# Causal mask in the last attention: two mask products on TensorE, or an addition on VectorE inside the row maximum

## The reference

```python
h = _rms(x, ln_w)
q = (h @ wq).reshape(B, S, NHEADS, HEAD_DIM); k = (h @ wk)...; v = (h @ wv)...
q, k = _rope(q, k)
scores = jnp.einsum('bqhd,bkhd->bhqk', q, k) / np.float32(np.sqrt(HEAD_DIM))
causal = jnp.tril(jnp.ones((S, S), bool))
scores = jnp.where(causal[None, None], scores, jnp.float32(-1e+30))
attn = jax.nn.softmax(scores, -1)
o = jnp.einsum('bhqk,bkhd->bqhd', attn, v).reshape(B, S, NHEADS * HEAD_DIM)
x = x + o @ wo
```

## Time and profile before

| | us |
|---|---|
| median of 3 runs | 4997.76 |
| lowest, highest | 4989.64, 5001.94 |
| span of the profiled execution | 4945.7 |
| what lies around the span (median less span) | 52.1 |
| PE, DVE, ACT, POOL busy in the span | 4241.6, 3176.8, 1929.8, 1642.4 |

### The profile page before, as it was taken

One profiled execution on the slowest core, in us unless ns is written; L12 is line 12 of the kernel. 1 busy time (PEld: TensorE's weight loads), 2 busy tenths in 40 slices (PEclk: granted clock), 3 DMA queues, 4 the chain that ended last, 5 costly groups with the idle time before them and its releaser, 6 DMA issues.

```text
span 4945.7 us, 68678 instructions
## 1 busy us (share of the span) xinstructions
PE 4241.6 (86%) x23426; PEld 2553.3 (52%) x23426; DVE 3176.8 (64%) x7341; ACT 1929.8 (39%) x4485; POOL 1642.4 (33%) x1384
## 2 busy tenths in 40 slices
PE   3698988888888895998858999999999999949985
PEld 1444544444454443775534555555555555547774
DVE  6788788878778775557635576666757666522223
ACT  0244435344443552322214455545555555511111
POOL 1000000000000002435004464546556554648885
PEclk6799999899999997999989999999999999979998
DMA  3211221211122106773041111111111111058888
GB/s 101 25 31 30 32 44 18 40 31 31 31 32 40 18 9 179 202 186 92 15 161 39 42 44 38 43 47 35 42 39 44 38 47 39 19 153 205 209 205 225
DMA packets 332115, 358.51 MB, mean 72 GB/s; under 512 B 177326, under 2 KB 257862, under 8 KB 330902
## 3 DMA queue, kind: packets, MB, share of 16 engines
q1 hardware_dynamic: 280888, 276.81, 21.6%
q0 software_dynamic: 47984, 76.34, 7.7%
q10 hardware_dynamic: 2898, 0.98, 0.1%
HBM read 212.35 MB, written 81.89 MB: 59 GB/s over the span
## 4 chain that ended last, share of the span: by engine, by line
PE 60%; DVE 22%; DMA 7%; ACT 4%; issue 3%; POOL 2%; SPq 1%; ACTq 0%; DVEq 0%; POOLq 0%
PE PS L2119 7%; DVE a_mm L1265 6%; PE PS L2104 6%; PE PS L2151 6%; PE PS L2134 5%; DMA e_xg<-hrow,e_mt 5%; PE PS L2161 4%; PE PS L914 3%; PE PS L854 2%; PE PS L1611 2%; PE PS L2122 2%; PE PS L881 2%; PE PS L719 2%; PE PS L2578 2%; PE PS L892 1%
## 5 line engine op out<-in xcount | busy, mean ns | idle before, releaser
L1265 DVE TENSOR_REDUCE a_mm<-PS 128x2 f32<-128x384 f32 (+4 forms) x1152 | 673.3, 610 | 232.6 <-PE PS L858 231.1
L2440 POOL TENSOR_TENSOR d_ef<-d_ef,d_zr 128x768 f32<-128x768 f32 (+3 forms) x512 | 640.1, 1258 | 449.9 <-DVE d_zr L2387 447.5
L1019 ACT ACTIVATE a_PT<-PS 128x512 f32<-128x512 f32 x896 | 514.9, 602 | 612.9 <-PE PS L892 397.0
L2207 ACT ACTIVATE d_ef<-PS,d_nm 128x128 f32<-128x128 f32 (+3 forms) x1024 | 529.3, 523 | 358.3 <-DVE d_zr L2387 298.6
L2378 DVE TENSOR_REDUCE d_nm<-PS 128x2 f32<-128x768 f32 (+3 forms) x512 | 419.3, 819 | 341.4 <-PE PS L2122 339.9
L1318 POOL DMA_INDIRECT list<-a_tok,slots x64 | 63.1, 986 | 1551.2 <-ACT a_PT L1019 1480.5
L2119 PE MATMUL PS<-d_k,d_q 64*128 64x128 f32 (+3 forms) x2048 | 421.3, 489 | 59.1 <-ACT d_ef L2207 41.2
L854 PE MATMUL PS<-a_K,a_Q 96*128 96x192 bf16 (+4 forms) x2048 | 420.0, 284 | 52.1 <-DVE a_mm L1265 22.9
L2134 PE MATMUL PS<-ident,d_ef 128*128 128x128 f32 x2560 | 369.2, 281 | 5.0 <-POOL d_ef L2440 4.1
L854 PEld LDWEIGHTS PS<-a_K,a_Q 80*128 80x128 bf16 (+1 forms) x2048 | 180.8, 103 | 357.3 <-DVE a_mm L1265 98.4
L2218 ACT ACTIVATE d_tf<-PS 128x512 f32<-128x512 f32 x320 | 190.7, 596 | 366.4 <-PE PS L2134 365.7
(11 more groups left out here) (347 smaller groups left out, 8104.0 us busy)
## 6 DMA issues: line engine op xcount, KB each, us to landing
e_we<-in_exp SPq DMA_DIRECT2D x79, 768.0 KB, 5.4
d_q<-d_rr SPq DMA_DIRECT2D x512, 64.0 KB, 2.0
bc_big<-in_exp SPq DMA_DIRECT2D x63, 384.0 KB, 4.3
d_k<-d_rr SPq DMA_DIRECT2D x256, 64.0 KB, 2.0
yrow<-bc_ob SPq DMA_DIRECT2D x63, 256.0 KB, 4.6
a_Q<-scr SPq DMA_DIRECT2D x384, 32.0 KB
scr<-a_qsp SPq DMA_DIRECT2D x24, 384.0 KB, 3.0
acc<-d_zero POOLq DMA_DIRECT2D x2, 4352.0 KB, 37.6
```

What stands on the lines that cost most here:

```text
L1019: e.activation(PT[:, 4 * (n % 2) + q4, :], RS.of(("exp", n, q4))[:, :], ACT.Exp, scale=S0).then_inc(act.sem, act.mark(("exp", n, q4)))
L1265: e.tensor_reduce(mm[:, i % 2, kind, c:c + len(gs)], RP.of(("top", b, u, kind, gs[0]))[:, 0:len(gs) * n].rearrange("p (g k) -> p g k", g=l ...
L2207: e.activation(ef[:, n % 7, r, 0:nk], S.of(("exp", n))[:, r, 0:nk], ACT.Exp, bias=nm[:, n % 7, r:r + 1], accum_out=zz[:, n % 7, r:r + 1]). ...
L2440: e.tensor_tensor(ef[:, n % 7, :, 0:nk], ef[:, n % 7, :, 0:nk], zr[:, n % 7, :].unsqueeze(2).to_broadcast([128, 2, nk]), ALU.mult).then_in ...
```

## The change

The mask moves from TensorE to VectorE. The tables for the query's rope are negated, so that the products give the negated scores. The two mask products and the identity `identb` are gone, and each score product now ends its group itself (`stop=True`) and signals. On VectorE one TENSOR_REDUCE over both heads becomes two `tensor_tensor_reduce`, one for each head: each adds the mask (0, or +1e30 where a key is later than the row) to the negated scores, writes the sum back to the same PSUM columns, and takes the minimum over the row into `nm`, which is the negated row maximum as before. The mask is now 512 columns wide, zero in the first 384, and its last `nk` columns are used. The exponential takes `scale=-1.0`. The buffer `tmp`, which nothing used, goes too.

```diff
-    c["rope1"] = np.stack([np.stack([t[:, f].T * np.float32(S2), t[:, f].T], 1) for t in (cos, sin)], 1)
+    c["rope1"] = np.stack([np.stack([t[:, f].T * np.float32(-S2), t[:, f].T], 1) for t in (cos, sin)], 1)
...
-    c["cmask1"] = np.where(np.arange(128)[None] <= p[:, None], 0.0, NEG).astype(bf)
+    c["cmask1"] = np.concatenate([np.zeros((128, 384)), np.where(np.arange(128)[None] <= p[:, None], 0.0, -NEG)], 1).astype(bf)
...
-            cmask = sb("cmask", [128, 128], BF16)
-            identb = sb("identb", [128, 128], BF16)
+            cmask = sb("cmask", [128, 512], BF16)
...
-                                     (identb, "identb"), (wo, "wo1"), (wg, "wgr"), (below, "below")):
+                                     (wo, "wo1"), (wg, "wgr"), (below, "below")):
...
                         e.matmul(p[:, r, 0:nk], q[rows, a % 2, hh, f, 128 * i:128 * i + 128],
-                                 kd[rows, hp // 2, 2 * (hp % 2) + hh, 0:nk], start=True, stop=False)
-                    for r in range(2):
-                        e.matmul(p[:, r, nk - 128:nk], identb[:], cmask[:], start=False, stop=True
+                                 kd[rows, hp // 2, 2 * (hp % 2) + hh, 0:nk], start=True, stop=True
                                  ).then_inc(pe.sem, pe.mark(("qk", n)))
...
-                                     bias=nm[:, n % 7, r:r + 1], accum_out=zz[:, n % 7, r:r + 1]
+                                     scale=-1.0, bias=nm[:, n % 7, r:r + 1], accum_out=zz[:, n % 7, r:r + 1]
...
                 def scores(n):
                     b, hp, i, hh, f = unit(n)
+                    nk = 128 * i + 128
                     e.wait_ge(pe.sem, pe.at(("qk", n)))
-                    e.tensor_reduce(nm[:, n % 7, :], S.of(("exp", n))[:, :, 0:128 * i + 128], AX, ALU.max, negate=True
-                                    ).then_inc(dve.sem, dve.mark(("max", n)))
+                    for r in range(2):
+                        masked = S.of(("exp", n))[:, r, 0:nk]
+                        e.tensor_tensor_reduce(masked, masked, cmask[:, 512 - nk:512], 1.0, BIG, ALU.add, ALU.min,
+                                               nm[:, n % 7, r:r + 1]).then_inc(dve.sem, dve.mark(("max", n)))
```

More of the change, by code:

```diff
@@ L1902, in phase_d @@
             oT = sb("oT", [128, 2, 512])
-            tmp = sb("tmp", [128, 256])
             zero = sb("zero", [128, 256])
```

## The result

| | before | after |
|---|---|---|
| median of the runs taken together (15 of each), us | 4998.05 | 4982.59 |
| lowest, highest | 4984.82, 5007.24 | 4970.15, 4990.3 |
| ratio of after to before, 95% interval | | 0.9969 [0.996, 0.9977] |

What follows compares the result with a forecast made beforehand. The prediction took TensorE to pace the last attention on the whole, VectorE 16 of 64 units a batch. TensorE's -31 us and VectorE's +26 us sum to -5 us, so 4992 us, range 4950 to 5035 us.

Steps and rivals of the forecast that it cites:

- the outcome given the best chance: Whole kernel: TensorE's gain and VectorE's cost cancel, a time between 4983 and 5013 us; chance 0.41.
- What bounds the kernel: Last attention: TensorE paces 48 of 64 units a batch, VectorE 16, in stretches with norms, routing and rope queued.
- TensorE's term: Mask products removed: 0.08 us a pair in 384 units paced by TensorE, -31 us (bounds 12 to 84 us gained).
- The sign I named for it: TensorE, units of 128 columns: transposes start 0.47 us after the score products instead of 0.55.
- rival B: TensorE's gain prevails: a pair is worth 0.12 us, giving 4965 us, or 0.22 us, giving 4927 us; chance 0.31.
- The bounds of 0.12 and 0.22 us: Higher values for a removed pair of mask products: 0.12 us by starts, 0.22 us by the chain.
- VectorE's term: Two additions replace one reduction: cost in 128 units paced by VectorE, less room for 16, +26 us (bounds +8, +62).
- x: VectorE's added time a unit: 0.07 us for a further instruction plus 0.08 for each accumulator reading, 0.23 us.
- my 112 units: Units that pay VectorE's added time, net: 128 paced by VectorE less 16 at the starts of stretches.
- Signals: Changed profile: VectorE's busy time up 118 us, TensorE's idle time a batch from 8.4 to about 12 us.
- C: Slower by VectorE's fixed costs in its own stretches: 0.55 us more a unit, +31 us, 5028 us; chance 0.18.
- D: VectorE runs the new instruction at half rate: 0.90 us more a unit, +70 us, 5068 us; chance 0.10.

Runs made afterwards that it cites:

- e11: The changed kernel with GpSimd's scaling cut to 2 columns a head, so probabilities aren't normalised: 4922.96 us.
- e1: The kernel before with both mask products left out and nothing in their place: 4967.1 us, stage 29.7 us shorter.
- e3: The changed kernel with the two mask products also kept on TensorE, so the mask is added twice: 5008.27 us.
- e6: The changed kernel with one more VectorE reduction in each unit, over 256 mask columns, its result unused: 5002.96 us.
- e7: The changed kernel with ScalarE taking all transpose copies in 6 of 32 pairs of units: 4980.31 us.
- e2: The kernel before with one mask product a unit instead of two (the first head's left out): 4983.47 us.

## Why the prediction held, point by point

The time lies in the stated range, but that range is 85 us wide. The forecast was -5 us, the result is -15.5; the outcome given the best chance, within 15 us, was missed by half a us. What held is the mechanism, a gain on TensorE in the quiet units against a smaller cost on VectorE in a busy stretch, and the size of the first term. The second term was twice too large.

- **What bounds the kernel: right, with one thing unseen.** TensorE on the whole, VectorE in a stretch of a batch; the quiet units gain 0.08 us each and the others lose. I counted both stretches alike, but nearly the whole loss is in units 27 to 36 (1.4 us a batch, 0.3 in units 11 to 17), though two of their three slices show TensorE busy for all of 12.50 us. What I didn't see is that VectorE's 9 to 11 busy us in those slices aren't all work: e11 shows about 9.5 us a batch as time held by GpSimd. I read a busy share as load.
- **TensorE's term: right in size and reason.** Forecast -31 us, measured -29.7 (e1) and 8 x -3.7 = -30 in the quiet units. As forecast, the first load behind the score products now begins where the mask's did, 0.42 us behind their start (0.50 before). The sign I named for it was wrong: the transposes start 0.43 us after the score products, as in rival B, not 0.47, but the open weight load takes 0.05 us of that back. The bounds of 0.12 and 0.22 us looked at the wrong rows: a start-to-start distance holds only if what follows doesn't itself get longer. In front of products with 64 output columns a pair does cost 0.21 us, in 4 of 64 units, which my 0.08 left out. With it 43 quiet units at 0.076 us and 4 at 0.21 make 4.1 us a batch, near the 3.9 of e1. The trace of before:

```profile
2830.30 0.28 PE L2122 MATMUL PS<-d_cmask,d_identb 128*128 128x128 bf16 x2
2830.51 3.65 PE L2151 MATMUL PS<-d_tf,d_vt 128*64 128x512 f32 x16
```

- **VectorE's term: right sign, twice too large.** Forecast +26 us, measured +13.3 (e3 by the stage, 7.5 by the time) and 8 x 1.7 = 14 us by stretches. The step that failed is x = 0.07 + 2 x 0.08: the first part should have been 0.13 (two fixed parts of 180 ns, less the one of 151 ns, less the 80 ns that the next instruction hides), and the reading of the accumulator should have been nothing. I priced it from ScalarE's row of 199 ns with 0.09 us until the next, the nearest row there was; VectorE's reading is hidden under the next instruction to within 0.01 us. With x = 0.13 my 112 units give 14.6 us and the sum -16, against -15.5 by the time and -19.1 by the stage.
- **The number of units: near, or too large.** 112 net in the forecast; 102 by e3's stage, 58 by its time, 80 by e6. That the number is near is partly luck, as the units that pay lie mostly in one of the two stretches from which it was counted.
- **Signals.** VectorE's busy time rose by 70 us over the span, not 118: of 145 us of reading rows most lie under other rows. The fixed part of an addition is 0.18 us, not 0.15; the columns cost the 1.04 ns forecast. TensorE's idle time a batch: about 12 forecast, 11.52 measured. The quiet stretches gave 3.7 us in some 159, which is 0.29 in 12.5, against 0.3 forecast. The second slot of S held: TensorE waits 58.1 us for the exponential over the stage (41.2 before), not above 100. From the waits of after:

```profile
PE PS L2117 <- ACT d_ef L2203: 58.1, 36, 3.1
```

- **The time around the span: wrong.** I set 52.1 us around the span. It is 1.4 us (4984.3 against 4982.8 in the profiled execution of after). The 52 us were the difference of an execution that was short ahead of the stage from the median. It fell out of the sum only because I used the difference. (The range's lower end is called halfway between 4965 and 4927; that would be 4946, not 4950.)
- **The rivals.** C's price (x = 0.55) and D (half rate) are out by the rows of 713 and 1227 ns. B's place as a result was half right: the time is at its edge, but not by its reason, since a pair is worth 0.08 us; the cause is the smaller x.

## What to carry to other kernels

Price an added instruction by the start of the one behind it, not by its own length: here the fixed part counted once for each instruction in the queue, and VectorE's accumulator reading counted nothing. What an instruction taken out is worth is told by how the next one's weight load stood beside it: it may have been hidden by what you remove. And ask of a busy engine whether its instructions are as long as elsewhere; if not, the gain lies with the engine that holds it (here 59.5 us of the stage against the change's 19.1; it is a ceiling, since e11 leaves GpSimd's work out and does not do it elsewhere).

## What the runs showed of the hardware

**VectorE is held while GpSimd works on SBUF.** After, a product over GpSimd and a scaling on VectorE, from the timeline:

```profile
2966.74 1.90 POOL L2439 TENSOR_TENSOR d_ef<-d_ef,d_zr 128x1024 f32<-128x1024 f32 x1
```
```profile
2967.36 1.44 DVE L238 TENSOR_SCALAR d_y<-d_xb,mv,rs 128x256 f32<-128x256 f32 x1
```

GpSimd's ends at 2968.64; VectorE's, which began meanwhile, at 2968.80, 1.44 us for what alone takes 0.41. All 28 such rows of the stage, before and then in e11 (shortest, median, longest in ns):

```profile
L238 DVE TENSOR_SCALAR d_y<-d_xb,mv,rs x28: 411/576/1489, 2700.2 to 4019.6; 128x256 f32<-128x256 f32 x28
```
```profile
L238 DVE TENSOR_SCALAR d_y<-d_xb,mv,rs x28: 411/414/642, 2747.2 to 4002.2; 128x256 f32<-128x256 f32 x28
```

The longest takes 1489 ns with the scaling in and 642 without, the median 576 and 414. Even operations on four columns are held, as in the timeline of e7, where GpSimd works through three scalings:

```profile
2890.61 4.32 POOL L2440 TENSOR_TENSOR d_ef<-d_ef,d_zr 128x768 f32<-128x768 f32 x3
2891.47 0.63 DVE L2235 TENSOR_TENSOR rs<-mv 128x4 f32<-128x4 f32 x1
2892.13 1.39 DVE L2237 TENSOR_TENSOR rs<-rs,mv 128x4 f32<-128x4 f32 x1
```

1.39 us where 0.16 is usual (2979.76 in e6). The Trainium skill ("SBUF — State Buffer", "Who interferes with whom") has this: VectorE instructions with two inputs in SBUF, or in a mode that uses both ports, share a pair of ports with GpSimd, and the later one is blocked. The trace agrees that such instructions wait (1.44 us for 0.41, 1.39 for 0.16); which ports do it no row shows. By the same section an instruction with one SBUF input, outside such a mode, isn't held. The change's own instructions, with scores in PSUM and only the mask in SBUF, show it: they last the same with the scaling in (after) and without it (e11):

```profile
L2377 DVE CUSTOM_DVE_ANT_0 PS<-PS,d_cmask x1024: 272/504/734, 2652.0 to 4345.0; 128x128 f32<-128x128 f32 x43, 128x384 f32<-128x384 f32 x43, 128x512 f32<-128x512 f32 x43, 128x256 f32<-128x256 f32 x42
```
```profile
L2377 DVE CUSTOM_DVE_ANT_0 PS<-PS,d_cmask x1024: 272/504/734, 2649.3 to 4281.8; 128x128 f32<-128x128 f32 x43, 128x384 f32<-128x384 f32 x43, 128x512 f32<-128x512 f32 x43, 128x256 f32<-128x256 f32 x42
```

**A large f32 weight load doesn't run ahead of score products.** Behind two products on halves of the array the load of the transposes begins with the first transpose (2814.87 and 2814.88); behind a mask product it began 0.05 us ahead. Over all 443 such places of the stage the medians are 2 ns after and 54 ns before. So a small bf16 product between them hides part of it: in the quiet units the first product taken out (e2) is worth 2.4 us a batch, and the one that is then left only 1.4. Whether the halves, the type or the width of the load decides, no run here parts.
